# First layer normalisation of a convolution and expert block: mean and variance on ScalarE instead of VectorE

## What is computed

```python
def _ln_c(v, eps=1e-06):
    m = jnp.mean(v, axis=-1, keepdims=True)
    s = jnp.var(v, axis=-1, keepdims=True)
    return (v - m) / jnp.sqrt(s + eps)

# convolution, on xn = _ln_c(x)
r = jax.nn.relu((xn @ Wr + br - mean) * rsqrt(var + 0.001) * gamma + beta)
w = r @ Ws + bs                    # 9 x 16 weights of each position
xi = xn @ Wi + bi                  # 128 channels of each position
out = sum(w * patches(xi), axis=-1)  # 3x3 neighbourhood
x = x + out
t = _to_tokens(x)
t = t + _L0_ffn_ref(_ln_t(t), ...)   # attention, routing, experts
```

## Time and profile before

| | |
|---|---|
| median of 3 runs | 2920.72 us (2920.6 to 2924.26) |
| profiled execution, span | 2918.8 us |
| VectorE busy | 2168.2 us, 74% |
| POOL busy | 1315.3 us, 45% |
| TensorE busy | 1017.2 us, 35% |
| ScalarE busy | 785.0 us, 27% |
| end of the convolution's last aggregation | 523.0 us |

### The profile page before, as it was taken

One profiled execution on the slowest core, in us unless ns is written; L12 is line 12 of the kernel. 1 busy time (PEld: TensorE's weight loads), 2 busy tenths in 40 slices (PEclk: granted clock), 3 DMA queues, 4 the chain that ended last, 5 costly groups with the idle time before them and its releaser, 6 DMA issues.

```text
span 2918.8 us, 22141 instructions
## 1 busy us (share of the span) xinstructions
PE 1017.2 (35%) x4867; PEld 685.7 (23%) x4867; DVE 2168.2 (74%) x4017; ACT 785.0 (27%) x1576; POOL 1315.3 (45%) x1234
## 2 busy tenths in 40 slices
PE   6777776599811110499333333310000000000000
PEld 3544454366511100266222222210000000000000
DVE  5999989999699974998888898856334313822888
ACT  3555544244411100144322222311000000000344
POOL 0000000000000007777777777778777777835750
PEclk8777666799955555699666666655555555555555
DMA  2222325992100011133231313142212113333676
GB/s 57 72 72 73 78 64 194 384 112 77 71 0 0 0 18 28 30 81 91 44 41 37 42 37 42 37 53 27 19 19 23 19 12 21 46 33 86 182 230 223
DMA packets 259502, 202.29 MB, mean 69 GB/s; under 512 B 101592, under 2 KB 207445, under 8 KB 258902
## 3 DMA queue, kind: packets, MB, share of 16 engines
q1 hardware_dynamic: 189766, 114.21, 17.5%
q0 software_dynamic: 46336, 44.61, 9.1%
q10 hardware_dynamic: 23314, 42.60, 4.6%
HBM read 94.51 MB, written 107.07 MB: 69 GB/s over the span
## 4 chain that ended last, share of the span: by engine, by line
POOL 40%; DVE 15%; issue 15%; PE 14%; DVEq 9%; DMA 3%; ACT 2%; ACTq 0%; POOLq 0%; SPq 0%
POOL sb_rows_g L770 38%; PE bank L1010 4%; DVE sb_xi L1656 3%; PE bank L1000 3%; DVEq L1672 2%; PE bank L926 2%; DVE sb_inv L1361 2%; DVEq L1392 1%; DVE sb_xi L1663 1%; DVEq L1382 1%; DVE sb_y_new L2146 1%; DVE sb_stats L1334 1%; PE bank L917 1%; POOL sb_agg L770 1%; DVEq L1387 1%
## 5 line engine op out<-in xcount | busy, mean ns | idle before, releaser
L770 POOL DMA_INDIRECT sb_rows_g<-scr_node,sb_srcs x1024 | 1107.3, 1081 | 312.1 <-issue 312.1
L1663 DVE TENSOR_TENSOR sb_xi<-sb_xi 128x512 f32<-128x512 f32 (+2 forms) x852 | 427.1, 568 | 46.8 <-ACT sb_xi L1159 33.0
L989 PE MATMUL bank<-sb_ident,sb_xi 128*128 128x128 f32 x448 | 99.5, 410 | 533.6 <-DVE sb_xi L1663 280.1
L770 POOL DMA_INDIRECT sb_hid_y<-scr_level,sb_row_at x8 | 9.3, 1163 | 597.2 <-DVE sb_row_at L1420 595.0
L1656 DVE TENSOR_TENSOR sb_xi<-sb_xi 128x1024 f32<-128x1024 f32 (+2 forms) x258 | 243.5, 944 | 28.2 <-ACT sb_xi L1164 9.5
L1000 PE MATMUL bank<-sb_tnT_in,sb_w 128*128 128x512 f32 x512 | 243.8, 630 | 58.0 <-DVE sb_sinks L1768 33.5
L1010 PE MATMUL bank<-sb_w,sb_hid_y 128*128 128x128 f32 x2048 | 262.6, 282 | 0.0
L1657 DVE TENSOR_TENSOR sb_xi<-sb_xi 128x1024 f32<-128x1024 f32 (+2 forms) x258 | 245.9, 953 | 0.0
L1010 PEld LDWEIGHTS bank<-sb_w,sb_hid_y 128*128 128x128 f32 x2048 | 238.2, 192 | 29.0 <-issue 29.0
L1182 ACT ACTIVATE sb_hid_y<-bank,sb_b1c 128x512 f32<-128x512 f32 x256 | 163.6, 691 | 239.2 <-PE bank L1000 237.5
L765 POOL DMA_DIRECT2D scr_adst_at_starts<-sb_zeros x1 | 1.1, 1057 | 487.3 <-DMA sb_xi<-in_L_ffn_edge_index 487.3
(11 more groups left out here) (337 smaller groups left out, 2175.8 us busy)
## 6 DMA issues: line engine op xcount, KB each, us to landing
scr_expert_out<-sb_y_new ACTq DMA_DIRECT2D x64, 512.0 KB, 3.8
sb_y_in<-scr_expert_out SPq DMA_DIRECT2D x32, 1024.0 KB, 6.8
scr_state<-sb_zeros POOLq DMA_DIRECT2D x6, 4096.0 KB, 55.9
sb_rows_g<-scr_node,sb_srcs POOLq DMA_INDIRECT x1024
scr_state<-sb_state SPq DMA_DIRECT2D x16, 768.0 KB, 7.0
scr_tnT<-sb_tnT SPq DMA_DIRECT2D x34, 256.0 KB, 2.0
sb_tnT_in<-scr_tnT ACTq DMA_DIRECT2D x34, 256.0 KB
sb_xa<-in_x SPq DMA_DIRECT2D x64, 128.0 KB, 2.5
```

The source lines that it names most:

```text
L770: pool.indirect_dma_start(to, None, table, bass.IndirectOffsetOnAxis(ap=index, axis=0), **kw).then_inc(s, 16)
L989: last = pe.transpose(bank[b][:, m * P:(m + 1) * P], src[:, (4 * b + m) * P:(4 * b + m + 1) * P], ident[:, :])
L1663: last = dve.tensor_tensor(vb[:, :, d, :, c], va[:, :, d, :, 0], va[:, :, d, :, 1], ALU.min if c == d else ALU.max)
```

## The change

VectorE no longer makes the statistics of `xa`. ScalarE makes them in `first_moments`: four copies of `xa` into the unused `xn` buffer with an accumulated sum each, a small multiplication that turns the sums into negative means, four squares with the mean as bias and an accumulated sum each, and the root. It waits for its own earlier instructions by a semaphore, `moments1`, at three places. `first_root` is gone; `first_moments` stands at the end of ScalarE's chunk, behind the node copy. On VectorE reciprocal and shift of the first normalisation move from the end of `conv_step(i)` (for chunk i+3) to behind its first product (for chunk i+2), beside those of the second. At the start, VectorE's loop over three chunks becomes one over two, and ScalarE makes the third chunk's moments after the copies of chunks 0 and 1.

```diff
-            def first_root(i):
-                act.wait_ge(stats1, i + 1)
-                act.activation(sd[:, 0], mv[:, 0, :, 1], ACT.Sqrt, bias=eps[:, 0:1]).then_inc(root1, 1)
+            def first_moments(i, v, loads):
+                act.wait_ge(xa_in[v], 32 * loads)
+                if some(i):
+                    act.wait_ge(scaled1, i)
+                if some(i - 1):
+                    act.wait_ge(turned1, i - 1)
+                for r in range(ROWS):
+                    last = act.activation(xn[:, v, r], xa[:, v, r], ACT.Copy, accum_out=mean1[:, 1, r:r + 1])
+                last.then_inc(moments1, 1)
+                act.wait_ge(moments1, 3 * i + 1)
+                act.activation(mean1[:, 0], mean1[:, 1], ACT.Copy, scale=-1.0 / C).then_inc(moments1, 1)
+                act.wait_ge(moments1, 3 * i + 2)
+                for r in range(ROWS):
+                    last = act.activation(xn[:, v, r], xa[:, v, r], ACT.Square, bias=mean1[:, 0, r:r + 1],
+                                          accum_out=spread[:, r:r + 1])
+                last.then_inc(moments1, 1)
+                act.wait_ge(moments1, 3 * i + 3)
+                act.activation(sd[:, 0], spread[:, :], ACT.Sqrt, bias=eps[:, 0:1], scale=1.0 / C).then_inc(root1, 1)
...
-                if more(i, 3):
-                    first_root(i + 3)
                 if some(i):
                     take_tokens(i - 1, 1 - u, turn if u else turn - 1)
                 if more(i, 2):
                     conv_copies(*after(q, c, 2), u)
                 if some(i):
                     node_copies(i - 1)
-
-            first_root(0)
+                if more(i, 3):
+                    first_moments(i + 3, 1 - u, turn + 2 + u)
+
+            first_moments(0, 0, 1)
             first_norm(0, 0)
-            first_root(1)
+            first_moments(1, 1, 1)
             first_norm(1, 1)
-            first_root(2)
             for u in (0, 1):
                 take_conv(u, u)
                 conv_copies(0, u, u)
                 if u == 0:
                     weight_copies(0, 0)
+            first_moments(2, 0, 2)
...
             def shifts(k):
-                dve.scalar_tensor_tensor(out=shift[:, k], in0=mv[:, k, :, 0], scalar=-1.0, in1=rstd[:, k],
-                                         op0=ALU.mult, op1=ALU.mult).then_inc((scaled1, scaled2)[k], 1)
+                if k == 0:
+                    dve.tensor_tensor(shift[:, 0], mean1[:, 0], rstd[:, 0], ALU.mult).then_inc(scaled1, 1)
+                else:
+                    dve.scalar_tensor_tensor(out=shift[:, 1], in0=mv[:, 1, :, 0], scalar=-1.0, in1=rstd[:, 1],
+                                             op0=ALU.mult, op1=ALU.mult).then_inc(scaled2, 1)
...
                 products(c, u, 0)
                 if some(i):
                     inverse(1, i - 1)
+                if more(i, 2):
+                    inverse(0, i + 2)
                 flush()
                 if some(i):
                     shifts(1)
+                if more(i, 2):
+                    shifts(0)
                 reduction(0)
                 products(c, u, 1)
-                if more(i, 3):
-                    dve.wait_ge(xa_in[1 - u], 32 * (turn + 2 + u))
-                    sums(0, xa[:, 1 - u])
-                flush()
-                if more(i, 3):
-                    moments(0, stats1)
+                flush()
...
-            for i in range(3):
-                dve.wait_ge(xa_in[i % 2], 32 * (i // 2 + 1))
-                sums(0, xa[:, i % 2])
-                flush()
-                moments(0, stats1)
+            for i in range(2):
                 inverse(0, i)
                 flush()
                 shifts(0)
```

More of the change, by code:

```diff
@@ L228, in metaformer_block @@
         shift = sb("shift", [P, 2, ROWS], F32, early)
+        mean1 = sb("mean1", [P, 2, ROWS], F32, early)
+        spread = sb("spread", [P, ROWS], F32, early)
         zeros = sb("zeros", [P, 1024], F32, early)
@@ L324, in metaformer_block @@
         win_placed, win_in = (sems(f"{n}0 {n}1") for n in ("win_placed", "win_in"))
-        (stats1, root1, scaled1, normed1, turned1, xnT_ready, r_psum, rT_ready, xi_psum, xi_ready,
+        (moments1, root1, scaled1, normed1, turned1, xnT_ready, r_psum, rT_ready, xi_psum, xi_ready,
          w_psum, w_ready, conv_done, root2, scaled2, normed2, turned2, tnT_ready,
          node_psum, node_ready) = sems(
-            "stats1 root1 scaled1 normed1 turned1 xnT_ready r_psum rT_ready xi_psum xi_ready "
+            "moments1 root1 scaled1 normed1 turned1 xnT_ready r_psum rT_ready xi_psum xi_ready "
             "w_psum w_ready conv_done root2 scaled2 normed2 turned2 tnT_ready "
@@ L1389, in conv_step @@
                 products(c, u, 3)
-                if more(i, 3):
-                    inverse(0, i + 3)
                 flush()
                 reduction(3)
-                if more(i, 3):
-                    shifts(0)
                 flush()
```

## The result

The changed kernel takes 3047.6 us (median of 4 runs, 3040.9 to 3050.0) beside 2920.7 us (4 runs, 2912.6 to 2924.3) of the kernel before: a ratio of 1.0426, 95% interval 1.0392 to 1.0460. The profiled execution has a span of 3048.2 us, 129.4 us more than before. The last addition of the convolution ends the comparison early: it starts at 650.02 us, before at 520.88, 129.1 later. All of the loss lies in the convolution.

The account below looks back on a forecast made before the run. The closed ScalarE-TensorE ring was taken to bound the convolution, VectorE's ring within 0.4 us of it. 15.17 - 0.22 + 4.2 + 0.17 = 19.3 us a chunk gave 112 us, plus 17 at the start: 3050 us, range 2990 to 3110.

Parts of the forecast that it names:

- The bound: Convolution: closed ScalarE-TensorE ring of 13.94 us, VectorE's 14.30; time between node copy and `xn` isn't absorbed.
- VectorE's gain: VectorE's ring in the convolution falls to some 13.2 us, worth only ScalarE's waits for the aggregation, 0.22 us a chunk.
- The price of the block: ScalarE, between node copy and root: 2.6 us with free accumulation, 4.2 us with 0.20 for each of eight.
- The clock mix: TensorE in the convolution: chunks never reaching the high clock stay at 4 of 27; more than 8 would refute it.
- Rival (a): TensorE: 20 of 27 chunks stay at the low clock instead of 4, 5.9 us more each, 3144 us; chance 0.08.
- The start: Before 74.3 us: later first blocks, and two chunks adding 2 x 4.4 us; together 17 us.
- (b): ScalarE's block: accumulation costs 0.6 us each if it must drain the engine, 93 us more, 3143 us; chance 0.05.
- (c): ScalarE absorbs the block in its waits for TensorE and VectorE's gain saves 30 us: 2891 us; chance 0.03.
- (d): Convolution: half of (c)'s saving, counted as no change, 2921 us; chance 0.02.

Follow-up runs that it names:

- plain_delay: The kernel before with 17 plain ScalarE copies put between node copy and root, VectorE keeping its statistics; 2990.3 us, ratio 1.0169.
- relief_alone: The kernel before without VectorE's four statistics and four aggregations of the first normalisation inside the chunks; 2932.2 us against 2933.0, ratio 0.9998.
- no_sums: The changed kernel with plain copies and squares, the accumulated sums left out and the root taken of a constant; 2988.4 us, ratio 1.0179.
- Short_ring: spread_out with weight copies behind the first normalisation, VectorE's first reciprocal and shift at the previous chunk's end, chunk 2's moments cut into the prologue; 2960.8 us, ratio 1.0102.
- short_ring_2: Short_ring with the weight copies moved on, behind the copy of the transposed `xn`; 2881.2 us, ratio 0.9832.
- spread_out: The changed kernel with ScalarE's block cut up and laid into its waits for TensorE, all computed; 2960.8 us, ratio 1.0078.
- before_warm: The kernel before with 14 thrown-away bf16 products on TensorE ahead of its wait for `xn`; 2928.6 us, ratio 1.0028.

## Why the prediction was right, and where its terms were off

**The bound.** Right. ScalarE and TensorE take turns in a closed ring, and time put between node copy and `xn` is paid nearly in full: plain_delay put in 3.39 us and the ring grew by 3.01, and 0.28 of the other 0.38 are a clock that rose earlier. In the changed kernel the ring grew by 3.36, where the block's 3.42 and 0.14 for `xn` give 3.56. The 0.2 that are missing have the size of the gone waits for the aggregation (0.22 by the prediction); which part is theirs wasn't measured.

**VectorE's gain.** Right as far as the runs can tell. Its busy time fell by 28.4 us (31 expected), and ScalarE's waits for the aggregation went. The 6 us that they were taken to be worth are too small for relief_alone to show in the time (0.9971 to 1.0026).

**The price of the block.** Mis-sized, within its bounds. The part without accumulation was sized at 2.6 and measured 2.68 us (no_sums). Copies and squares take 297 and 389 ns; the Trainium skill's formula in "ScalarE: Activation LUTs", section "What ACT_TABLE_LOAD costs", gives 293 and 386, and the trace agrees. The term that was off is the accumulation: assumed 0.20 us each, measured 0.09. The instruction is there and takes 0.187 us, but half of it lies over its neighbours on both sides, not on one. The block is 3.42 us instead of 4.2: 27 x 0.78 = 21 us too much. `xn` starts 320.34 - 319.43 = 0.91 us after the root's start, 0.14 more than before where 0.17 was expected.

**The clock mix.** Wrong. It was assumed to stay at 4 low chunks of 27, and the text itself named more than 8 as what would refute it; there are 9. That cost 28.6 us which the sum didn't have. Rival (a), at 20 low chunks and 94 us, was the right mechanism at under a third of its size, but not for the reason given. The inference drawn from the Trainium skill's page "TensorE: Matmul & The Clock Gate", section "Part 1: The HAM clock gate", that more idling can only add low chunks, isn't borne out: 6.2 us of idling a chunk went with none, 3.1 us with 4, 7.7 us with 8. Short_ring and short_ring_2 idle the same 2.3 us a chunk (61.4 us in 27 waits each), and have 10 and none.

**The start.** Mis-sized. 17 us were expected before the stretch; the first node copy is 6.3 us later and the part behind the 28th 3.7 us longer, 10 together. The first `xn` came at 16.63 (expected 17.4), and the copy L1053, now L1070, 2.2 us later instead of 3.8, for the block was sized too dear. That `xn` of chunk 2 came 7.45 later, where 8.0 were expected, is in part luck: chunk 1 is low throughout in the changed kernel and not before. From there to the first node copy the changed kernel has one more block and is still 1.1 us quicker, because chunk 2 is low throughout in the kernel before and not in this one. And of the two chunks added with 4.4 us each only one lies before the stretch, the other behind it.

So the total, 3050 against 3047.6, came out close by luck: against the sum the ring measured 21 us less, the low chunks 29 more and the start 7 less, and these nearly cancel. The direction and the ring carry the forecast; its agreement to 3 us does not.

**Rivals (b), (c), (d).** Accumulation needs no draining of the engine: (b) is out. ScalarE doesn't absorb the block where it stands, the node copy's wait is unchanged; cut into the waits (spread_out) it does, and yet nothing is gained on the kernel before. Of (c)'s 30 us, short_ring_2 reached 18 by its ring, with the order of ScalarE changed as well; the rest of what it gained is the clock's.

**Open.** What decides how many chunks stay at the low clock. The counts against the ring are 13.66: 0, 14.03: 5, 14.21: 10, 14.31: 8, 14.34: 4, 14.47: 3, 17.06 and 17.08: 0, 17.55: 10, 17.70: 9, 19.37: 8. They don't follow the length in one direction, nor the idling; two kernels with nearly the same ring (17.06 and 17.08 us) agree, though what fills ScalarE's block differs. Low chunks also come at regular steps over parts of the stretch (in the changed kernel 23.5 and 17.5 us in turns). And the place in the chunk at which the clock rises wanders: in three chunks of the kernel before that follow one another, the first group of L926 takes 1.65, 1.04 and 0.94 us (at 198.87, 213.84 and 228.08). Both suggest that it matters where a chunk falls in time against something with a beat of its own. That is argued, not shown.

## What to carry to other kernels

Read busy shares last: first close the ring of the engines that wait for each other, and ask on which side of it an added instruction stands; the same ten activations made the ring 3.4 us longer behind the node copy and no longer in ScalarE's waits. Where two rings are within a few per cent of each other, do both parts separately and together, since here neither alone moved the time beyond its noise. And where TensorE's clock moves, compare the rings of chunks at the high clock and count the low ones apart: here 0.4 us more a chunk came with ten more low chunks, some 60 us beside its own 12, and a gain of 39 us was more than half a matter of low chunks.

## What the runs showed of the hardware

An accumulated output makes ScalarE run a second instruction, the reading of the accumulator; these are its groups in the changed kernel over the stretch (count, busy us, mean ns):

```profile
L1060 ACT ACTIVATE sb_xn<-sb_xa,sb_mean 128x128 f32<-128x128 f32 x108 | 42.0, 389 | 0.9
L1054 ACT ACTIVATE sb_xn<-sb_xa 128x128 f32<-128x128 f32 x108 | 31.9, 297 | 0.0
...
L1054 ACT ACTIVATION_READ_ACCUMULATOR sb_xn<-sb_xa 128x1 f32 x108 | 20.2, 187 | 0.0
```

It is 187 ns long and 0.09 us net per accumulating activation in a row of them. The other surprise is the clock: with two more copies on ScalarE, 0.40 us a chunk, TensorE went from 0 low chunks of 27 to 10, and its mean granted clock from 0.79 to 0.63. Filling its idle time doesn't prevent them: in all nine low chunks of before_warm the filler ran at the high level (1.69 us for 14 products), and the clock fell behind it.
